# Six attention layers and a routed feed-forward on one core: routing tables in eight pieces, two-tile statistics, a last product in two banks

## The reference

```python
h = take(tok_W.T, x)                       # 16 x 256 tokens, rows of 256 floats
x_ = layernorm(h)
for l in range(6):                         # attention layers, out of softmaxed q and k
    y = layernorm(x_, gamma[l], beta[l]); q, k, v = split(y @ w_qkv[l], 3)
    q, k = softmax(q, axis=1), softmax(k, axis=2)
    context = einsum('bic,bjc->bij', k, v)
    x_ = einsum('bic,bij->bjc', q, context) @ w_out[l] + b_out[l] + x_
h = h + x_
z = layernorm(h)
gate = z @ gate_w                          # 8 experts, the best 2, softmax over these
out = sum_e swiglu_e(z) * w_e + swiglu_shared(z)   # swiglu: silu(z@w1) * (z@w2) @ w3
return h + out
```

## Time and profile before

| | us |
|---|---|
| median of 3 runs (1444.32 to 1445.19) | 1444.95 |
| the profiled execution's own time | 1447.14 |
| its span, first to last instruction | 1445.4 |
| TensorE busy | 1262.4 (87%) |
| VectorE busy | 1046.6 (72%) |
| GpSimd busy | 959.4 (66%) |
| ScalarE busy | 830.8 (57%) |

### The profile page before, as it was taken

The page is one execution under the profiler, slowest core; times in us unless marked ns, Lnnn a source line. Parts: engine busy times, 40 slices in busy tenths (PEclk is TensorE's granted clock), DMA queues, the critical chain, the costliest instruction groups (busy, mean ns, idle before and its releaser), DMA issues. The chain is left out here.

```text
span 1445.4 us, 37041 instructions
## 1 busy us (share of the span) xinstructions
PE 1262.4 (87%) x10992; PEld 1054.0 (73%) x10993; DVE 1046.6 (72%) x2675; ACT 830.8 (57%) x2286; POOL 959.4 (66%) x958
## 2 busy tenths in 40 slices
PE   4400499999999999999999999988998999999996
PEld 3400388888888888888888888854564888888885
DVE  3246789998898899889989989866765455545553
ACT  2230278878777877888788777767552232332321
POOL 0057889889888888898898889836752143343433
PEclk8755799999999999999999999998999999999998
DMA  9994264543464345335433445654444344544441
GB/s 318 384 319 133 53 117 95 131 111 67 87 134 81 58 110 133 62 68 138 98 65 58 94 109 89 104 85 108 140 123 148 58 65 61 73 62 68 63 64 14
DMA packets 354415, 157.13 MB, mean 109 GB/s; under 512 B 283953, under 2 KB 338737, under 8 KB 354353
## 3 DMA queue, kind: packets, MB, share of 16 engines
q1 hardware_dynamic: 321090, 117.99, 36.0%
q0 software_dynamic: 20064, 25.32, 9.9%
q10 hardware_dynamic: 13200, 13.11, 2.6%
HBM read 44.50 MB, written 42.64 MB: 60 GB/s over the span
## 5 line engine op out<-in xcount | busy, mean ns | idle before, releaser
L731 PE MATMUL bank<-hT,Wc 128*128 128x256 f16 x2304 | 285.9, 275 | 88.3 <-DMA hT<-hhl 76.1
L731 PEld LDWEIGHTS bank<-hT,Wc 128*128 128x128 f16 x2304 | 226.3, 98 | 116.7 <-issue 88.7
L691 POOL DMA_INDIRECT out_rows<-h0b,payin x78 | 121.9, 1562 | 209.7 <-DVE h0b L1471 150.3
L828 PE MATMUL bank<-xTg,Wall 128*128 128x256 f16 x1872 | 211.0, 273 | 0.0
L828 PEld LDWEIGHTS bank<-xTg,Wall 128*128 x1872 | 182.6, 98 | 22.4 <-issue 0.8
L596 POOL TENSOR_TENSOR h0b<-h0b,rows 128x512 f32<-128x512 f32 x96 | 121.8, 1269 | 98.7 <-issue 53.3
L1096 ACT ACTIVATE silu<-bank 128x512 f32<-128x512 f32 x110 | 65.5, 596 | 176.4 <-PE bank L828 150.6
L1399 DVE SCALAR_TENSOR_TENSOR gT<-bank,silu 128x512 f32<-128x512 f32 x110 | 76.0, 691 | 111.4 <-ACT silu L1096 110.6
L731 PE MATMUL bank<-Wc,MT 128*128 128x256 f16 x1152 | 143.8, 275 | 9.2 <-DVE MT L1262 9.2
L731 PE MATMUL bank<-khl,eqT 128*128 128x256 f16 x1152 | 142.0, 273 | 5.7
L731 PE MATMUL bank<-Wc,hT 128*128 128x256 f16 x1152 | 143.1, 275 | 0.0
(11 more groups left out here) (150 smaller groups left out, 2591.6 us busy)
## 6 DMA issues: line engine op xcount, KB each, us to landing
Wall<-in_L_tok_W SPq DMA_DIRECT2D x25, 512.0 KB, 7.8
emb_rows<-Wall ACTq DMA_DIRECT2D x25, 512.0 KB, 11.4
Wall<-in_L_ffn_ew SPq DMA_DIRECT2D x24, 512.0 KB, 4.0
Wc<-Wn SPq DMA_DIRECT2D x48, 128.0 KB, 2.3
Wst<-in_L_attn_w_qkv SPq DMA_DIRECT2D x12, 384.0 KB, 3.6
h_rows<-Wall SPq DMA_DIRECT2D x4, 1024.0 KB, 4.8
X<-h_rows POOLq DMA_DIRECT2D x8, 512.0 KB, 6.7
out_rows<-X SPq DMA_DIRECT2D x8, 512.0 KB
```

The source lines that it names most:

```text
L691: pool.indirect_dma_start(out=out_rows, out_offset=bass.IndirectOffsetOnAxis(ap=got(j % PAYS, w, 0, i32), axis=0), in_=yout[j % 2][:, w, : ...
L731: last = mm(to, lhs(a, k, o), moving, start=(i == 0 and k == 0), stop=(i == 2 and k == 1))
L828: last = mm(to, cols(a, e, 2 * k + w, (2 * half + c) * P, P), moving, start=(n_ == 0), stop=(n_ == 5))
```

## The change

1. `tables()` becomes eight functions. `counts` runs in step 6 ahead of `gate_shared(6, 2)`, `pair_counts` and `pair_ends` behind `gate_shared(6, 2)` and `(6, 3)`. In step 7 follow `pair_bases` and `pair_experts` behind the first share, `pair_starts` behind the second, and `pair_places` and `pair_words`, which release SyncE and TensorE, behind `gate_shared(7, 2)`.
2. `stats_of` takes a range of tiles: behind items 88 to 95 VectorE does two tiles of groups 0 to 3. Groups 4 and 5 move behind `rank(0)` and `rank(1)`.
3. `high(g)` is split into `normed(g)` and `high(g)`: normalize behind items 90, 92, 94, cast behind 91, 93, 95 for groups 0 to 2. The two halves of `h0b` change roles. `nmr` gets memory of its own, `root(0)` moves behind GpSimd's item 89, and GpSimd's list behind the loop is in another order: `root(5)` stands ahead of `scatter_x(0)`, where `low(3)` stood.
4. The shared expert is loaded in two steps of SyncE instead of three and split in items 82 to 87.
5. In the last pair down(37) goes between the two up halves, and down(38) puts its row halves into two banks; each is scaled and added to the output by itself.

```diff
             pair(eng.snap(l * (2 * quarter) + b + quarter), EXPERT, eng.snap(l * quarter + b + XEARLY // 2))
-    start = (ITEMS - AHEAD - XPER) // 2
+    start = (ITEMS - AHEAD - XPER) // 2 - 1
...
         pair(h, PLAIN)
-    if unroll == 0:
+    if not unroll:
...
             pair(eng.snap(b + start), LAST, eng.snap(b + (XALL - XPER) // 2))
+        with eng.Fori(start + XPER // 2, (ITEMS - AHEAD) // 2) as h:
+            pair(h, PLAIN)
     else:
-        for t in range(ITEMS - AHEAD - XPER, ITEMS - AHEAD):
-            one(t, t % 2, LAST, t + XALL - ITEMS + AHEAD)
+        for t in range(2 * start, ITEMS - AHEAD):
+            c = t - 2 * start
+            one(t, t % 2, LAST if c < XPER else PLAIN, c + XALL - XPER if c < XPER else None)
...
             install(l, 3)
-        if l == DEPTH - 1 and -1 <= i < 2:
+        if l == DEPTH - 1 and -1 <= i < 1:
...
                     sp.wait_ge(ready, 32 * DEPTH)
-            load_expert(E, i + 1)
+                load_expert(E, 0)
+                load_expert(E, 1)
+            else:
+                load_expert(E, 2)
...
-item_loop(pool, one, AHEAD, between={g - 7: partial(first_root, g) for g in range(1, 4)} |
-          {ITEMS - 12: add_first} | {ITEMS - 12 + 2 * g: partial(add_h0, g) for g in range(1, 4)}, unroll=XPER)
...
+item_loop(pool, one, AHEAD, unroll=True,
+          between={g - 7: partial(first_root, g) for g in range(1, 4)} |
+          {ITEMS - 12: add_first, ITEMS - 10: partial(add_h0, 1), ITEMS - 8: partial(add_h0, 2),
+                   ITEMS - 7: partial(root, 0), ITEMS - 6: partial(add_h0, 3)})
...
     pool.wait_ge(s_fxhi, g + 1)
-    pool.tensor_tensor(xhl(g % ROWS, 1), h0b[:, g % 2, :, :], xhl(g % ROWS, 0), ALU.subtract).then_inc(s_fxlo, 1)
+    pool.tensor_tensor(xhl(g % ROWS, 1), h0b[:, 1 - g % 2, :, :], xhl(g % ROWS, 0), ALU.subtract).then_inc(s_fxlo, 1)
...
 add_h0(4)
-root(0)
 root(1)
+low(0)
 add_h0(5)
-low(0)
...
 low(1)
+add_h0(6)
 root(3)
-add_h0(6)
-root(4)
...
 add_h0(7)
+root(4)
+low(3)
 root(5)
-low(3)
...
 for j in range(PAIRS):
-    pool.wait_ge(s_yout, j + 1)
+    if j < PAIRS - 1:
+        pool.wait_ge(s_yout, j + 1)
...
     for w in range(2):
+        if j == PAIRS - 1:
+            pool.wait_ge(s_oend, w + 1)
...
             for c in range(HC):
-                last = mm(pb[4 + p][:, w * D:(w + 1) * D], gThl[:, p, a, c, w * P:(w + 1) * P], cols(b, e, KH * 2 + c // 2, c % 2 * D, D),
+                to = pb[5 - p if w else 4 + p][:, 0:D] if apart else pb[4 + p][:, w * D:(w + 1) * D]
+                last = mm(to, gThl[:, p, a, c, w * P:(w + 1) * P], cols(b, e, KH * 2 + c // 2, c % 2 * D, D),
...
                 n_ += 1
-    last.then_inc(s_y, 1)
+        if apart:
+            last.then_inc(s_yend, 1)
+    if not apart:
+        last.then_inc(s_y, 1)
...
         up_slots(j, p, 0, at[i], nth[i // 2])
+        end = last and i == n - 1
...
             down_shared(SHP - 2)
+        elif end:
+            down(pair[i] + SHP, 1 - p, prev)
...
             down_shared(SHP - 1)
-        else:
+        elif not end:
...
     if last:
-        down(pair[n] + SHP, (n - 1) % 2, prev)
+        pe.wait_ge(s_yout, PAIRS - 1)
+        down(pair[n] + SHP, (n - 1) % 2, prev, True)
...
-def high(g):
-    x4 = slice(GT * g, GT * (g + 1))
+def normed(g):
     act.wait_ge(s_nmr, g + 1)
-    if g == 0:
+    if g == 1:
...
     for t in range(GT):
-        last = A(h0b[:, g % 2, t, :], X[:, GT * g + t, :], ACT.Identity, bias=nmr[:, GT * g + t:GT * g + t + 1],
+        last = A(h0b[:, 1 - g % 2, t, :], X[:, GT * g + t, :], ACT.Identity, bias=nmr[:, GT * g + t:GT * g + t + 1],
...
     last.then_inc(s_xf, 1)
+def high(g):
...
             act.wait_ge(ready, 32 * DEPTH)
+        act.wait_ge(s_xlo, XALL)
...
-item_loop(act, one, 2, between={ITEMS - 4: lambda: high(0), ITEMS - 2: lambda: high(1)})
+item_loop(act, one, 2, between={
+    **{ITEMS - 6 + 2 * g: partial(normed, g) for g in range(3)}, **{ITEMS - 5 + 2 * g: partial(high, g) for g in range(3)}})
...
 high_shared(0, 0)
-high(2)
...
 share_exp(1)
+normed(3)
...
     if g + 3 < NG:
+        normed(g + 3)
...
         last.then_inc(s_amv, 1)
-item_loop(dve, one, AHEAD, between={**{2 * g - 7: partial(first_norm, g) for g in range(1, 4)},
-                                    **{ITEMS - 6 + g: partial(stats_of, g) for g in range(6)}})
+item_loop(dve, one, AHEAD, unroll=True, between={
+    **{2 * g - 7: partial(first_norm, g) for g in range(1, 4)},
+    **{ITEMS - 8 + i: partial(stats_of, i // 2, 2 * (i % 2), 2 * (i % 2) + 2) for i in range(8)}})
...
-def tables():
+def counts():
...
+def pair_counts():
...
+def pair_ends():
...
+    return at
+def pair_bases(at):
...
-    wide = [P, WORDS, E]
+wide = [P, WORDS, E]
+def pair_experts():
...
-    V.tensor_reduce(pair_e[:, :], past[:, :, :], AX.X, ALU.add)
+    link(V.tensor_reduce(pair_e[:, :], past[:, :, :], AX.X, ALU.add))
+def pair_starts():
...
+def pair_places():
...
+def pair_words():
...
 rank(0)
+stats_of(4)
...
 rank(1)
+stats_of(5)
...
     share(2 * g - 2, 0)
+    if g == NG - 1:
+        pair_bases(ends)
+        pair_experts()
...
         rank(g + 1)
-    if g + 1 == NG - 1:
-        tables()
+    if g == NG - 2:
+        counts()
+    if g == NG - 1:
+        pair_starts()
     gate_shared(g, 2)
+    if g == NG - 2:
+        pair_counts()
+    if g == NG - 1:
+        pair_places()
+        pair_words()
     gate_shared(g, 3)
+    if g == NG - 2:
+        ends = pair_ends()
...
     dve.wait_ge(s_prob, j + 1)
-    dve.wait_ge(s_y, j + SHP + 1)
+    end = isinstance(j, int) and j == PAIRS - 1
+    if not end:
+        dve.wait_ge(s_y, j + SHP + 1)
...
     for w in range(2):
-        last = V.tensor_scalar(yout[p][:, w, :], pb[4 + p][:, w * D:(w + 1) * D], prob[:, p, w:w + 1], None, ALU.mult)
-    last.then_inc(s_yout, 1)
+        if end:
+            dve.wait_ge(s_yend, w + 1)
+            V.tensor_scalar(yout[p][:, w, :], pb[5 - p if w else 4 + p][:, 0:D], prob[:, p, w:w + 1], None, ALU.mult)\
+                .then_inc(s_oend, 1)
+        else:
+            last = V.tensor_scalar(yout[p][:, w, :], pb[4 + p][:, w * D:(w + 1) * D], prob[:, p, w:w + 1], None, ALU.mult)
+    if not end:
+        last.then_inc(s_yout, 1)
...
 glow(SHP, 0, 1)
-for j in range(1, PAIRS):
+for j in range(1, PAIRS - 1):
...
     weigh(j - 1, 1 - j % 2, (j - 1) % PAYS, (j - 1) // PAYS + 1)
+gate(SHP + PAIRS - 1, 0)
+weigh(PAIRS - 2, 1, (PAIRS - 2) % PAYS, (PAIRS - 2) // PAYS + 1)
+gate(SHP + PAIRS - 1, 1)
```

More of the change, by code:

```diff
@@ L100, in tower @@
         rstd = sb("rstd", [P, NT], f32)
+        nmr = sb("nmr", [P, NT], f32)
         h0b = sb("h0b", [P, 2, 4, D], f32)
@@ L206, in tower @@
             xT[i] = sb(f"xT{i}", [P, GT, 2, KH, P], f16, ffn)
-        nmr = sb("nmr", [P, NT], f32, ffn)
         xrow[2], xT[2] = sb("xrow2", [P, GT, ROW], f32, ffn), sb("xT2", [P, GT, 2, KH, P], f16, ffn)
@@ L265, in tower @@
         s_pay = [sem(f"s_pay{i}") for i in range(PAYS)]
+        s_yend, s_oend = sem("s_yend"), sem("s_oend")
         s_yout, s_sadd, s_is0, s_part, s_prob = (sem(n) for n in ("s_yout", "s_sadd", "s_is0", "s_part", "s_prob"))
@@ L301, in tower, with item_loop @@
         PLAIN, CUT, EXPERT, LAST = range(4)
-        def item_loop(eng, one, lead, other=True, between={}, unroll=0):
+        def item_loop(eng, one, lead, other=True, between={}, unroll=False):
             def pair(h, kind, c=None):
@@ L831, in up, with down @@
                 last.then_inc(s_h12, 1)
-            def down(i, p, e):
+            def down(i, p, e, apart=False):
                 pe.wait_ge(s_glo, 2 * i + 2)
@@ L1028, in high @@
                     act.wait_ge(s_xT[(g - ROWS) % RING], 16 * GT * ((g - ROWS) // RING + 1))
-                A(xhl(g % ROWS, 0), h0b[:, g % 2, :, :], ACT.Copy).then_inc(s_fxhi, 1)
+                A(xhl(g % ROWS, 0), h0b[:, 1 - g % 2, :, :], ACT.Copy).then_inc(s_fxhi, 1)
             def one(t, p, kind, c):
@@ L1224, in _, with stats_of @@
             first_norm(0)
-            def stats_of(g):
+            def stats_of(g, first=0, end=GT):
                 dve.wait_ge(s_h0add[g], 16)
-                half = GT * (g % 2)
-                for t in range(GT):
+                half = GT * (1 - g % 2)
+                for t in range(first, end):
                     V.bn_stats(stats[:, half + t, :], X[:, GT * g + t, :]).then_inc(s_st, 1)
-                dve.wait_ge(s_st, NT + GT * (g + 1))
-                for t in range(GT):
+                dve.wait_ge(s_st, NT + GT * g + end)
+                for t in range(first, end):
                     V.bn_aggr(mv[:, GT * g + t, :], stats[:, half + t:half + t + 1, :]).then_inc(s_stat, 1)
```

## The result

The changed kernel takes 1454.01 us (median of 4 runs, 1451.08 to 1458.40) where the kernel before took 1444.63, measured beside it: a ratio of 1.0068, 95% interval [1.0042, 1.0094]. That is 9.4 us slower. The forecast was slower, by 3.7 us, with 1453.0 as its upper end; the direction was right, the size was not.

The account below looks back on a forecast made before the run. TensorE was taken to set the pace nearly everywhere, so only its idle time could be won. Terms -1.0 + 6.0 - 1.0 + 0.5 - 0.8 = +3.7 us on 1444.95 gave 1448.6 us, range 1440.2 to 1453.

Parts of the forecast that it names:

- The new wait: Behind the last attention item: root(5) delays group 0's scatters, ScalarE's group 4 cast and a gated product; +6.0 us.
- That would bring TensorE forward by 2 to 3 us at 991: Behind the last attention item: the gain from two vanished xT waits, expected to be given back within one group.
- Two waits for xT go: Behind the last attention item: two TensorE waits for xT vanish because low(1) and low(2) are ready earlier.
- The eqT transposes that a GpSimd accumulate DMA delays stay where they are: In the last attention items: claimed no shift of these delayed transposes; no term of its own in the sum.
- the first two steps: The last attention items (-1.0 us) and the lost xT waits, bringing TensorE forward 2 to 3 us at 991.
- some 9 and 5 us earlier: Behind the last attention item: how much sooner low(1) and low(2) on GpSimd would be ready.
- The last items: Attention items 88 to 95: smaller statistics and normalize lumps, -1.0 us; bounds +2 and -4, the latter if the clock holds.
- The meetings of low(g) with VectorE: Shared expert: GpSimd shifts 5 us against TensorE, low(6) misses VectorE's subtraction, low(5) half meets; -1.0 of 0 to -2.5.
- The tables: Before the first expert pair: the 5.56 us stall becomes a 5.5 us wait for transposes; +0.5 us, bounds -2.5 and +2.5.
- Rival (2): The tables' stall really goes if addresses are ready by 1107: -7.9 instead of +0.5, total 1440.2 us; chance 0.10.
- The tail: Last expert pair: earlier scatters and output by halves, against 2.9 us idle before the last down; -0.8 us.
- Rivals (1) and (3): (1) smaller scatter 0 wait, covered by gains: about 1445.5, chance 0.28; (3) scatter 0 delays nobody: 1440.6, chance 0.10.

Follow-up runs that it names:

- t5_h06: The changed kernel with add_h0(6) moved back behind root(3) and low(2); ratio 1.0031 to the kernel before.
- t1_tables: The kernel before with only the routing tables split into eight pieces; ratio 1.0006 to the kernel before.
- t8_early: t1_tables with pair_bases, pair_experts, pair_starts and pair_places moved ahead of the next to last shared addition; ratio 0.9961 to the kernel before.
- t2_tail: The kernel before with only the last pair's new order and two banks; ratio 0.9982 to the kernel before.
- t4_order: The changed kernel with scatter_x(0) ahead of root(5) in GpSimd's list, nothing else; ratio 1.0041 to the kernel before.
- t12_best: t9_both with add_h0(6) moved from in front of root(4) to behind low(2); ratio 0.9999 to the kernel before.
- r8_early: t8_early measured once more, unedited; 1441.43 us, ratio 0.9972 to the kernel before.
- t3_front: The changed kernel with the tables in one piece and the old tail, so only the changeover differs from before; ratio 1.0069 to the kernel before.
- t9_both: t8_early with the last pair's new order and two banks; ratio 0.9984 to the kernel before, 0.9963 when measured again.

## Why the prediction was right in direction and wrong in size

**The new wait (term +6.0, bounds 2 to 9): right in mechanism, and nearly in its own size.** Forecast was an idle stretch of some 6 us and 2.3 us for the fallen clock; measured were 6.89 and 2.4 (5.17 us for twelve, 2.76 at full clock). Over this stretch the forecast went from 3.5 us ahead to 5.0 behind, a swing of 8.5; measured was 1.9 behind to 11.7 behind, a swing of 9.8. The first scatter left at 1002.05 where I had 996.4, 5.6 us later than forecast: rank(1) ended at 997.6 instead of 992.6, and 0.6 us lie between root(5) and the scatter.

**The step that failed: "That would bring TensorE forward by 2 to 3 us at 991".** The reason given, "Two waits for xT go", came true: the waits of 3.44 and 2.66 us are gone. What was left out is the DMA that moved with low(1) and low(2). add_h0(6) was now ahead of root(3) and left at 960.79, inside the transposes of group 0, so that a third wait for xT arose where none had been, 3.12 us and a fallen clock. At 992.94 TensorE was 1.9 us late instead of 2 to 3 early. The prediction said "The eqT transposes that a GpSimd accumulate DMA delays stay where they are": it knew that additions delay transposes, but the sum has no term for the one that moved beside the xT transposes. t5_h06 shows its price, 5.3 us by the ratios and 6.9 by the traces. It shows also that the rest of this part of the forecast was sound: with this one call moved back TensorE is 4.5 us ahead at 991, where the first two steps make 3.5, and 4.7 behind after the long wait, where the forecast made 5.0.

In the walk of the two traces, the changed kernel is 11.7 us late behind the long wait, a miss of 6.7 against those 5.0. The meetings below add 1.0, the tables and the tail take 0.2 off: 7.5, about the 7.6 between the trace's 11.3 and the forecast's 3.7.

That low(1) and low(2) would be ready "some 9 and 5 us earlier" was not met either: low(1) started at 958.73 against 964.32, low(2) at 978.61 against 978.93. low(2) stands behind root(3), which waits for the statistics behind item 95, and that item was held up by the new wait; in t5_h06 low(2) starts at 971.88. Of the two waits, that for group 2's xT is gone only because TensorE came later to it; in t5_h06, where TensorE comes early, it is there with 3.72 us.

**The last items (term -1.0): right, by parts of which one was overlooked.** The kernel is 1.1 us ahead at 962.75 and 1.6 ahead when it comes to the first xT. The shorter lumps of VectorE did shorten the wait before item 94's product (1.84 us against 2.26), and the clock held behind it, as the lower bound had foreseen. The longer wait for eqT, 3.25 us against 1.02 at 945.03, with products at the lower clock behind it, took back most of that; that the sum came out is in part luck, since the clock held at this product in some kernels with the old changeover as well (below).

**The meetings of low(g) with VectorE (term -1.0): wrong, measured 0.** The waits are 2.01 and 0.60 us, against 1.91 and 0.60 before, and the stretched subtraction takes 3.09 us at 1039.86 where it took 2.99. The prediction shifted GpSimd by 5 us "against TensorE", but its own terms had TensorE 5 us late too, by the same scatters. From its first scatter to low(5) GpSimd works without a pause of more than half a microsecond: low(5) starts 37.7 us behind the first scatter in the kernel before (1028.52) and 38.2 behind it in the changed one (1040.26). So the scatters' delay of 11.3 us reaches low(5) whole, TensorE and VectorE are 11.7 us late behind the wait that the same scatters make, and the engines meet again.

**The tables (term +0.5): right.** The wait moved to the transposes of the first pair, 5.21 us idle and 5.21 us for 24 products of 256 columns where 2.78 is full clock. The walk gives +0.4 (11.7 to 12.2), t1_tables 1.0006. pair_at came at 1124.3 in the changed kernel, 12.0 us later than the forecast's 1112.3, much as everything else. Rival (2) named the point from which it decides, addresses by 1107 in the time of the kernel before; t8_early had them at 1100 and was 5.6 us faster than the kernel before (4.0 when measured again), against the 7.9 that rival gave; 2.52 us of wait for the last gated product remain there. The load of an address, for which the page "DMA: Bandwidth & Descriptors" of the Trainium skill (section "Latency and other measured facts") has a floor of about 600 ns, took 268 to 310 ns, so the term needed nothing for it.

**The tail (term -0.8): right.** 0.9 us in the changed kernel, 0.8 in t2_tail; the last down started behind 2.95 us idle (2.9 forecast) and the clock fell. The rule of the Trainium skill that the prediction weighed (page "TensorE: Matmul & The Clock Gate", Part 1: the throttled clock is the default and activity releases it) agrees with both tails: 4.52 and 4.57 us for 24 products that take 2.78 in full clock. Below there are gaps as long behind which the clock did not fall.

**Rivals (1) and (3).** Both needed the statistics of group 5, and with them scatter 0, to come early. They did not, and even with scatter_x(0) ahead of root(5) a third group of statistics held the masks for 3.42 us (t4_order).

## What to carry to other kernels

When an order on a queue is edited, list every DMA that moves with it and lay each beside the transfers of other queues at its new time: a 512 KB addition beside transposes that TensorE needs cost 5.3 us here, nearly as much as the wait that I had priced at 6.0. An edit that splits a lump pays only if its last piece, the one on which the next stage waits, also moves earlier: the tables in pieces won nothing until the piece with the addresses stood in VectorE's own idle time. And lumps of an engine's work add up where they are put down: of the three groups of statistics put in a row behind rank(1), the first held root(5), and all three together held the masks.

## What the runs showed of the hardware

The clock of TensorE does not follow from the length of a gap alone. The same gap of 2.26 us at the same product was followed by 2.46 us for twelve products in the kernel before, by 2.03 in t12_best and by 1.48 (full clock) in t8_early. One kernel alone shows it too: r8_early is t8_early unedited, and there they took 1.90. The row of t8_early:

```profile
957.11 1.48 PE L731 MATMUL bank<-Wc,MT 128*128 128x256 f16 x12 [2.26 <-DVE MT L1262]
```

And t3_front ran twelve 128x512 products at full clock (2.76 us) straight behind 3.69 us idle, where the changed kernel took 5.30 behind 3.12:

```profile
969.17 2.76 PE L866 MATMUL bank<-xT,Wall 128*128 128x512 f16 x12 [3.69 <-DMA xT<-xrow]
```

A gap here is thus worth itself, or itself and what the lower clock costs (some 2.5 us for twelve 128x512 products), and one trace does not tell which.

In two of the series, those with medians of 1451.2 and 1456.1 us for the kernel before, TensorE had gaps in the shared expert for which the trace names no releaser, 4 to 11 us in all; in the traces of those at 1444.6 to 1444.9 there were none. The four series of experiments ran on four chips, and the gaps are on two of them. From the waits of t9_both (976 to 1125 us) and its timeline:

```profile
PE bank L884 <- issue: 5.4, 9, 1.2
```

```profile
1079.92 0.27 PE L884 MATMUL bank<-Wall,gThl 128*128 128x256 f16 x1 [0.44 <-issue]
1080.63 2.24 PE L884 MATMUL bank<-Wall,gThl 128*128 128x256 f16 x19 [0.45 <-issue]
```

One product, 0.44 us of nothing, and on. What TensorE lacks there is not shown.
